# Macaron block in float32 on one core: six weight halves loaded behind two gathers, weight subtractions behind a tile's bias, second tile's transposes inside the first product

## The reference

```python
def _L0_ffn_ref(x, W_gate, b_gate, W_e, b_e):
    logits = x @ W_gate + b_gate
    _, top_idx = jax.lax.top_k(logits, TOP_K)
    y_all = jax.nn.relu(jnp.einsum('bsd,edh->bseh', x, W_e) + b_e)
    y = jnp.take_along_axis(y_all, top_idx[..., None], axis=2)
    return y.mean(axis=2)
...
x = x + 0.5 * _L0_ffn_ref(_layernorm(x, axis=-1), ...)
x = x + _L0_attn_ref(_layernorm(x, axis=-1), ...)
x = x + 0.5 * _L0_ffn_ref(_layernorm(x, axis=-1), ...)
```

## Time and profile before

| what | us |
|---|---|
| median of 3 executions | 304.62 (302.92 to 304.64) |
| the profiled execution | 304.77 |
| its span from the first instruction to the last | 303.0 |
| PE busy / DVE busy / POOL busy / ACT busy | 241.8 / 168.8 / 130.7 / 103.0 |

### The profile page before, as it was taken

One profiled execution on the slowest core, in us unless ns is written; L12 is line 12 of the kernel. 1 busy time (PEld: TensorE's weight loads), 2 busy tenths in 40 slices (PEclk: granted clock), 3 DMA queues, 4 the chain that ended last, 5 costly groups with the idle time before them and its releaser, 6 DMA issues. The chain is left out here.

```text
span 303.0 us, 4792 instructions
## 1 busy us (share of the span) xinstructions
PE 241.8 (80%) x1278; PEld 181.2 (60%) x1279; DVE 168.8 (56%) x385; ACT 103.0 (34%) x183; POOL 130.7 (43%) x144
## 2 busy tenths in 40 slices
PE   6677269587799999939999997639999999999400
PEld 2343048465688888717868765224888888888300
DVE  4579536565543444488658656883343443444691
ACT  1988312434234233201425434211224234233100
POOL 4200623364656664345672400006366665663440
PEclk9999859979999999987999997956999999999955
DMA  7999976323434544444121011104344534455893
GB/s 256 390 396 404 392 271 226 103 85 105 143 119 151 170 137 138 139 139 141 34 104 42 30 70 70 71 1 131 105 150 154 173 133 134 128 173 184 283 323 117
DMA packets 22787, 49.35 MB, mean 163 GB/s; under 512 B 4332, under 2 KB 4972, under 8 KB 22512
## 3 DMA queue, kind: packets, MB, share of 16 engines
q1 hardware_dynamic: 13712, 26.55, 24.2%
q0 software_dynamic: 7360, 20.46, 20.7%
q10 hardware_dynamic: 1696, 2.11, 2.0%
HBM read 34.42 MB, written 18.35 MB: 174 GB/s over the span
## 5 line engine op out<-in xcount | busy, mean ns | idle before, releaser
L454 POOL DMA_INDIRECT z_dram<-yrow,place x46 | 46.8, 1016 | 65.9 <-ACT yrow L585 56.6
L446 POOL DMA_INDIRECT xg<-xn_dram,tok x46 | 50.6, 1101 | 50.7 <-DVE tok L1094 31.7
L1106 DVE TENSOR_TENSOR xt_lo<-tp_ps,xt_hi 128x512 fp32r<-128x512 f32 x46 | 31.8, 692 | 67.5 <-ACT xt_hi L578 66.3
L585 ACT ACTIVATE yrow<-ypre 128x512 f32<-128x512 f32 x46 | 29.1, 632 | 106.4 <-DVE ypre L1114 71.9
L757 PE MATMUL tp_ps<-ident,xg 128*128 128x128 f32 x184 | 29.0, 282 | 8.5 <-DMA xg<-xn_dram,tok 6.5
L757 PEld LDWEIGHTS tp_ps<-ident,xg 128*128 128x128 f32 x184 | 23.5, 145 | 16.2 <-DMA xg<-xn_dram,tok 7.9
L775 PE MATMUL y_ps<-whi,xt_hi 128*128 x96 | 29.1, 426 | 3.7 <-ACT xt_hi L578 3.4
L578 ACT ACTIVATE xt_hi<-tp_ps 128x512 fp32r<-128x512 f32 x46 | 26.7, 580 | 15.6 <-PE tp_ps L757 15.6
L775 PE MATMUL qk_ps<-whi,xt_hi 128*128 x88 | 26.0, 417 | 4.7 <-ACT xt_hi L578 2.6
L775 PE MATMUL y_ps<-wlo,xt_hi 128*128 x96 | 27.1, 406 | 0.0
L775 PE MATMUL y_ps<-whi,xt_lo 128*128 x96 | 26.7, 401 | 0.0
(11 more groups left out here) (127 smaller groups left out, 349.9 us busy)
## 6 DMA issues: line engine op xcount, KB each, us to landing
raw<-in_L_ffn_W_e_dram SPq DMA_DIRECT2D x16, 512.0 KB, 11.4
z_rows<-z_dram SPq DMA_DIRECT2D x8, 512.0 KB, 3.4
x<-in_L_attn_x_dram SPq DMA_DIRECT2D x8, 256.0 KB, 3.9
be_bc<-in_L_ffn_b_e_dram SPq DMA_DIRECT2D x2, 1024.0 KB, 10.9
xn_dram<-xn ACTq DMA_DIRECT2D x8, 256.0 KB, 2.0
z_last<-z_dram SPq DMA_DIRECT2D x4, 512.0 KB, 5.9
out_dram<-x SPq DMA_DIRECT2D x8, 256.0 KB, 4.0
xn_dram<-xn SPq DMA_DIRECT2D x4, 256.0 KB, 10.3
```

Source lines behind the costliest of these rows:

```text
L446: pool.indirect_dma_start(out=xg[:, t % XG, :], out_offset=None, in_=xn_dram[f][:, :], in_offset=bass.IndirectOffsetOnAxis(ap=tok[:, t:t + ...
L454: pool.indirect_dma_start(out=z_dram[f][:, :], out_offset=bass.IndirectOffsetOnAxis(ap=place[:, t:t + 1], axis=0), in_=yrow[:, t % YB, :], ...
L585: act.activation(yrow[:, t % YB, :], ypre[:, t % 2, :], ACT.Relu, scale=HALF_MEAN).then_inc(yrow_made, 1)
L1106: dve.tensor_tensor(xt_lo[:, t % 2, :], tp_ps[(n0 + t) % 2][:], xt_hi[:, t % 2, :].bitcast(F32), ALU.subtract).then_inc(xt_made, 1)
```

## The change

Five places. The first three are in layer 0 alone.

- SP issues halves 8 and 9 behind the first biases as before, then waits for gathers 0 and 1, and then issues halves 10 to 15, the second biases and, without the wait for the third gather, the attention's weights.
- DVE makes `place` and `tok` before `eid` (it was the other way round in layer 0), and in the loop it does tile t's bias before the subtractions of that tile. `LO_IN_TILE` is now [2, 2, 2, 2, 1, 2].
- ACT makes 10 halves of `whi` ahead of the loop, not 11, and six in it. PE has 16 dummy matmuls behind the list, not 10.
- In both layers three more dummy matmuls stand behind the transposes of tile 0.
- In both layers the transposes of tile 1 stand inside product 0, between its eighth and ninth matmul, and not ahead of it.

```diff
         SUM_END = [3, 5, 7]
-        WARM = [10, 10]
+        WARM = [16, 10]
...
-        HI_AHEAD = 11
+        HI_AHEAD = 10
         LO_AHEAD = 5
-        LO_IN_TILE = [2, 2, 2, 2, 1, 1, 1]
+        LO_IN_TILE = [2, 2, 2, 2, 1, 2]
+
+        LOAD_AHEAD = 10
...
             load_be(0)
-            for n in range(E, 2 * E):
+            for n in range(E, LOAD_AHEAD):
+                load_half(n)
+            for s in range(2):
+                sp.wait_ge(gathered[s], 16)
+            for n in range(LOAD_AHEAD, 2 * E):
                 load_half(n)
             load_be(1)
-            sp.wait_ge(gathered[XG - 1], 16)
...
-                def product(t, tile_no, copied, made, read):
+                def product(t, tile_no, copied, made, read, between=None):
...
                         if rows is xt_lo:
+                            if between is not None:
+                                between()
                             pe.wait_ge(xt_made, made)
...
                 def tile(t):
-                    if t + 1 < NS:
-                        if t:
-                            transposes(t + 1, landed(t + 1), xt_made, f * NS + t)
-                        else:
-                            transposes(t + 1, landed(t + 1), tp_copied, n0)
-                    product(t, t, n0 + t + 1, f * NS + t + 1, f * NS + t - 1 if f or t >= 2 else None)
+                    if t and t + 1 < NS:
+                        transposes(t + 1, landed(t + 1), xt_made, f * NS + t)
+                    product(t, t, n0 + t + 1, f * NS + t + 1, f * NS + t - 1 if f or t >= 2 else None,
+                            None if t else lambda: transposes(1, landed(1), tp_copied, n0))
 
                 transposes(0, landed(0), tp_copied, n0 - 1)
+                warm_up(3)
                 pe.wait_ge(eid_made, f + 1)
...
                 row_hots(f, B - 1)
-                if f == 0:
-                    tile_experts(f)
                 dve.wait_ge(list_done, f + 1)
...
                 dve.tensor_single_scalar(tok[:], place[:], T - 1, ALU.bitwise_and).then_inc(tok_made, 1)
-                if f:
-                    tile_experts(f)
+                tile_experts(f)
...
                     if t + 1 < NS:
                         lo_rows(t + 1, n0 + t + 2)
+                    bias(t, t, f * NS + t + 1, f * NS + t - 1 if f or t >= 2 else None)
                     if f == 0 and t < len(LO_IN_TILE):
                         for _ in range(LO_IN_TILE[t]):
                             split_lo(dve, halves.pop(0), lo_made)
-                    bias(t, t, f * NS + t + 1, f * NS + t - 1 if f or t >= 2 else None)
```

## The result

The changed kernel takes 291.99 us (median of 4 executions, 290.66 to 293.10) against 304.55 us before. The ratio is 0.960, with a 95% interval of 0.955 to 0.964: 4.0% faster, 12.6 us. The prediction was 290.0 us with a range of 286.5 to 296.0. The same kernel, measured again beside its variants on two other chips, gave ratios of 0.952 and 0.958. The profiled execution took 290.66 us, 14.1 us less than the one of before.

The account below looks back on a forecast made before the run. PE was taken to idle at layer 0's start, its gather slow beside SP's loads, then to wait on a 5.69 us cycle per tile. Start 6.8 plus loop 9.0 minus 1.0 gave 14.8 us off 304.77: 290.0 us, range 286.5 to 296.0.

Parts of the forecast that it names:

- The list to the gather's issue: Layer 0's start: with tok first, gather 0 is issued at 31.14 us, 0.37 us earlier.
- Gather 0's landing: Layer 0's start: landing 2.36 us behind POOL's end, as in layer 1, so tile 0 is transposed at 35.0, not 38.84 us.
- rival B: Layer 0's start: gather 0 is slow by itself, free DMA saves only 0.7 us; 294 us in all, chance 0.09.
- POOL under DVE's subtractions: Layer 0's start: the part of gather 0 under DVE's subtractions slowed by 1.87/1.05, POOL's end at 32.65 us.
- The clock: PE before tile 0's transposes: a 1.2 us gap leaves the clock at 2.4 GHz; a fall would cost 1.8 us.
- The start term: Layer 0 up to the first bias: 40.3 us where it was 47.09, a saving of 6.8 us.
- The loop's pace: Layer 0's loop: 3.49 us a tile on DVE with the bias ahead of the subtractions; the loop saves 9.0 us.
- What may take some of it back: Layer 0's loop: late halves, biases and gathers beside each other cost 1.0 us, bounds 0 and 3.
- Rival A: Layer 0's loop: the halves starve gathers 3 to 5, product 2 begins near 50 us; 295 us in all, chance 0.10.
- signs of being wrong: Trace marks named beforehand: DMA releasing transposes 3 to 5, transposes at 37.8 us, waits for raw, biases over 4 us apart, 6 us products.
- C: Layer 0's loop: ACT's and DVE's weight work keeps the pace at 4.3 us a tile, not 3.5; 295 us, chance 0.08.

Follow-up runs that it names:

- e6: The changed kernel without SP's wait for gathers 0 and 1, all halves issued at once: 293.27 us, ratio 0.965.
- e1: The kernel before with only the gathers' part: halves 10 to 15 behind gathers 0 and 1, tok before eid, ten weight copies ahead: 302.71 us, 0.994.
- e2: The kernel before with only DVE's loop order changed, bias ahead of the weight subtractions, with the new counts per tile: 295.66 us, ratio 0.971.
- e3: The kernel before with only PE's part: 16 and 3 dummy matmuls, tile 1's transposes inside product 0: 304.58 us, ratio 0.998.
- e10: The changed kernel with the subtractions of halves 3 and 4 moved from ahead of tile 0's rows to behind them: 293.46 us, ratio 0.963.
- e11: The changed kernel with the changes of e9 and e10 together: 288.54 us, ratio 0.947.
- e5: The changed kernel with 10 dummy matmuls instead of 16 and without the three behind tile 0's transposes: 291.68 us, ratio 0.956.
- e9: The changed kernel with half 10 ahead of SP's wait, second biases behind half 12, attention's weights behind the last gather: 290.11 us, ratio 0.951.

## Why the prediction was right

The time, the sign and both mechanisms were right; one term was too small by a factor of three and another error stood beside it. That the total came so near is in part luck, as the last point says.

- **The list to the gather's issue**: 0.37 us predicted, 0.39 measured.
- **Gather 0's landing.** I took the row of layer 1 and not rival B's, 2.36 us behind POOL's end against bounds of 2.36 and 5.46. It was 34.67 - 32.30 = 2.37. e6, in which only SP's wait is gone, shows that the loads do it (6.33 us from issue against 3.55 to 3.67 in the changed kernel), and e1 (3.66) and e2 (7.57) agree. From POOL's end to T it is 5.15 to 5.70 us beside the loads (before, e2, e3, e6) and 2.37 to 2.49 in the ten others: they cost 2.7 to 3.3 us. By the rule of taking turns in the Trainium skill ("DMA: Bandwidth & Descriptors", section "SWDGE vs HWDGE vs iDMA"), as I had read it, they would cost 0.7 us, an estimate. Rival B is out; whether the queues take turns no run shows.
- **POOL under DVE's subtractions.** This step failed. I had scaled the remaining part of a gather by 1.87/1.05. Gather 0 took 1.18 us and not 1.51, and gather 1, wholly behind the start of the three subtractions, 3.25 and not 1.75: it ended 0.84 us behind their end at 35.02 us. In each of the 14 traces gather 1 ended 0.82 to 0.84 us behind the end of the subtractions, three of them or (e10, e11) one, and the earlier trace rows showed it already: 33.69 + 1.74 = 35.43 against 31.12 + 3.48 = 34.60. e10 shows that they were the cause. The error moved SP's release from 37.2 to 38.16 us.
- **The clock** stayed at 1.00, as predicted. e5 shows what the dummies are worth at the start, 1.2 us, and that the loop as it stands gives 0.9 of it back.
- **The start term**, 6.8 us: 6.5 measured (47.09 to 40.58 us), by two errors that partly cancel. T came at 34.67 us and not 35.0, but from T to the first bias it took 5.91 us and not 5.3: from tile 1's subtraction to the bias alone 1.06 (39.52 to 40.58) and not 0.61.
- **The loop's pace**, 3.49 us: 3.64. The path named was the right one, DVE's own sum; the handoff from the rows' subtraction to the bias is 0.78 us (49.30 to 50.08) and not the 0.61 that I had taken from another handoff on that engine. In e11, where no load is late, the stretch takes 25.26 us against 24.4: 0.9 us in all.
- **"What may take some of it back"**, 1.0 us, is the mis-sized term. It measured 28.28 - 25.26 = 3.0 us (2.2 and 3.4 in the two repeats), of it 2.3 half 10, 0.6 the second biases and 0.2 gather 6. For half 10 I had allowed 0 to 0.5 us: it landed 5.8 us behind SP's release and not 4.7 and was issued 1.0 us later than I had it. A 512 KB load with five more behind it isn't a `z_rows` load of the earlier trace rows; the page of the profile before gave 11.4 us as the weights' median and I took the friendlier row. The second biases I had counted as bytes but not by the time at which they are wanted, though DVE wants them in tile 4. And I had weighed gather 5 and not gather 6, the one that PE waited for, 7.2 us behind its issue. My bounds of 0 and 3 did reach the measured value. Rival A described the same thing, larger than it was. Of the signs of being wrong, those of C did show, ACT waiting for `raw` and two of the first five biases over 4 us behind the one before, and product 7 began at 65.71 us and not at 61.5 to 62.5; but it was loads that were late, not ACT and DVE that were too slow.
- **What covered the miss.** Loop and start gave 11.6 us where the sum had 14.8, 3.2 short, and 2.5 us came in the profiled execution outside it, 1.7 of them no doing of the change. So the profile's 290.66 us stands 0.7 over the forecast by luck; the median stands 2.0 us over it.

Two things stay open. Layer 1's beginning takes 11.6 to 12.1 us from its first gather to its second bias in the variants that have PE's part, and 12.05, 12.26 and 13.73 in the three kernels without it (before, e2, e1), so its gain of 0 to 0.4 us isn't shown. And how a gather of 256 KB comes to need 7 to 9 us beside loads was not taken apart: the runs show which transfers stood beside it, not what held it.

## What to carry to other kernels

A transfer that is moved out of one engine's way lands in another's: list every transfer that is wanted in the next 20 us with the time at which it is wanted, and count behind the release the queue ahead of each, before the wait is called free. Here the wait won 3.9 us at the start and lost 3.0 in the loop. Only e11 kept both, in which each late load had its own place (the first half ahead of the wait, the biases by the tile that needs them, the attention's weights behind the last gather) and the wait itself ended 2 us sooner. On an engine that serves a chain and a background task, put the chain's instruction first: that one swap, which moved no byte and saved no instruction, was worth 2.9% alone.

## What the runs showed of the hardware

- POOL's time for an indirect gather isn't slowed evenly by DVE's subtractions of two operands in memory. Begun 1.06 us into three in a row (3.47 us) it took 3.25 us; begun 0.15 us before the end of a single one (e10) 0.98; in all 14 traces this gather ended 0.82 to 0.84 us behind the end of the subtractions. In the loop a gather takes 0.97 to 0.98 us in the new order, where it begins up to 0.1 us ahead of the pair or between two pairs, and took 2.0 in the old, where it began 0.06 us into the pair; the scatter is 1.68 to 1.71 us where it was 1.01 to 1.02. Which of the two transfers meets the subtractions decides which is slow; the sum is 2.7 us a tile, and was 3.0.
- A gather of 128 rows of 2 KB was there 3.55 to 3.67 us behind its issue with a quiet DMA system (DMA share 0.23) and 6.3 to 7.6 us beside a full queue of SP's loads (1.06), and in the loop up to 9.3 us (gather 4 of e9). Its own 256 KB are 0.7 us at 389 GB/s, an estimate.
- The granted clock fell after an idle gap of PE of 2.40 us in e5 and did not after 1.04 to 1.16 us in the changed kernel, nor after the 1.63 us that PE waits in its loop for half 10 (1.00 from 45 to 50 us); it fell too behind the gap of 2.30 us in e10's loop.
